# The second copy of each unit's head outputs, moved from ScalarE to a transfer inside SBUF

## The chip, the cores and the metric

The kernel runs on one NeuronCore of a Trainium2 chip. The metric is the device time of one launch in microseconds (us). A core has five instruction streams that run beside each other and meet at semaphores: TensorE (PE in the rows; its weight loads are PEld), VectorE (DVE), ScalarE (ACT), GpSimd (POOL) and SyncE (SP), which here only issues transfers (DMA).

## What is computed

Four sequences of 512 tokens by 256 features pass through four residual layers: latent attention, a feed-forward layer with weights from a 16-entry table, a state-space layer with a scan along the tokens, and the feed-forward layer again. The change is in the attention. Cut to it:

```python
# 16 heads of 128 columns, rank-64 keys and values shared by all heads (absorbed in the kernel)
scores = einsum('bqhd,bkhd->bhqk', q, k) * scale          # causal mask
probs  = softmax(scores)
out    = einsum('bhqk,bkhd->bqhd', probs, v)              # head outputs
x      = x + out.reshape(bs, seq_len, 16 * 128) @ wo.T    # output projection
```

Products run in a reduced fp32 format (fp32r), and each operand that needs more precision is kept as a high part, which is the rounded value, and a low part, which is the rest.

## The kernel before

The attention works in **units**. A unit is one tile of 128 query tokens by one group of G = 4 heads; a sequence has 4 token tiles, so 16 units, and the four sequences have 64. Units 0 to 3 of a sequence belong to token tile 0 and see one block of 128 keys, units 4 to 7 (tile 1) see two blocks, and so on to four in tile 3. Below, "tile 0 of batch 1" means units 0 to 3 of the second sequence.

The order is written out by hand in **slots**. In slot s every engine works on several units at once: `q_up` for unit s, `q_transpose` for s - 2, `scores` and `exp` for s - 3, `p_transpose` for s - 4, `values` for s - 5 and `project` for s - 6 (functions `pe_slot`, `act_slot`, `dve_slot`). The functions wait for each other only by semaphores, and each engine takes its own list strictly in order.

For one unit the steps around the change are these. TensorE transposes the probabilities (`p_transpose`, L1573) once ScalarE has normalised all of them (`normalise`, L866). ScalarE and VectorE split each transposed block into high and low parts (`pt_high` L875, `pt_low` L1205), and `values` (L1587 and L1590) multiplies them by the values into the PSUM bank `bank[6]`: 128 rows by 4 heads by 128 tokens. The matrix `v_hl` holds the high part of the 64 value columns beside the low part, so that rows 0 to 63 of the bank are the product with the high part, rows 64 to 127 that with the low part.

Then the head outputs are split. `out_high` on ScalarE copies the whole bank as `o_a` (L881) and rows 0 to 63 once more as the first half of `o_b` (L883). `out_low` on VectorE puts rows 0 to 63 of the bank less `o_a`, the low part, in the second half of `o_b` (L1211). `project` on TensorE (L1600, L1602) multiplies `o_a` by the weights `wo_a` and `o_b` by `wo_b`. `o_a` and `o_b` have two buffers each, used in turn (`n % 2`). The next unit's first `values` waits for `out_low`, since it overwrites the bank.

`out_high` stands in the middle of `act_slot`: behind it come the squares for the next batch's norm (in tile 0 of the first three batches; L825), the third and fourth `exp` of a later unit (L846), `q_copy` (L853) and the `normalise` calls for which the next `p_transpose` waits. `project` stands near the end of the slot after the one in which `out_high` ran. GpSimd is expanding the table weights all through the attention (L782, L788). SyncE has loaded the inputs by then; its only work during the attention is four loads of state-space weights (`ssm_nat`, L734 to L738), which wait for the last batch's token steps.

Of the kernel before, what the change touches and what calls it, by code (L numbers as in the profile page):

```python
# [4 lines left out]
F32 = mybir.dt.float32  # L5
# [6 lines left out]
P = 128  # L12
BATCH, SEQ, DIM = 4, 512, 256
TB = SEQ // P
CK = DIM // P
HEADS, NOPE, ROPE, DV = 16, 128, 64, 128
QR, KR = 192, 64
# [3 lines left out]
UNITS = TB * (HEADS // G)  # L21
# [59 lines left out]
def token_count(b, k):  # L81

    return 1 + 14 * b + k - 4 * (b - (k == 0)) if b else 1 + k
# [24 lines left out]
def build(nc, x_in, wq_down, wq_up, wq_rope, q_norm_w, wkv_down, kv_norm_w, wkv_up, wk_rope, wo,  # L108
# [3 lines left out]
    with ctx:  # L112
# [89 lines left out]
        o_a = r2("o_a", [P, 2, G, P], F32R)  # L202
        o_b = r2("o_b", [P, 2, G, P], F32R)
# [13 lines left out]
        ssm_nat = nc.alloc_sbuf_tensor_at("ssm_nat", [P, 3, CK, DIM], F32, offset=r2_at)  # L217
# [13 lines left out]
        bank = [nc.alloc_psum_tensor(f"bank{i}", [P, 512], F32) for i in range(8)]  # L231

        def sem(name):
            return ctx.enter_context(nc.semaphore(name))
# [4 lines left out]
        dnat_in, ssm_in, wkn_in, wv_in, wqr_in, wo_in = (  # L239
            sem(n) for n in ("dnat_in", "ssm_in", "wkn_in", "wv_in", "wqr_in", "wo_in"))  # L240
# [17 lines left out]
        at_mm, at_hi, at_lo = sem("at_mm"), sem("at_hi"), sem("at_lo")  # L258
# [3 lines left out]
        recip_s, norm_a, norm_d = sem("recip_s"), sem("norm_a"), sem("norm_d")  # L262
        pt_mm, pt_hi_s, pt_lo_s, pv_mm = sem("pt_mm"), sem("pt_hi_s"), sem("pt_lo_s"), sem("pv_mm")
        o_hi_s, o_lo_s, y_mm = sem("o_hi_s"), sem("o_lo_s"), sem("y_mm")
        x_add, f_add, s_add = sem("x_add"), sem("f_add"), sem("s_add")

        gu_mm, silu_s, hf_s, hhi_s, hlo_s, dn_mm = (
# [432 lines left out]
        @block.sync  # L700
        def _(sp_):
            xr = x_in.rearrange("b (t p) d -> b p t d", p=P)
            outr = out.rearrange("b (t p) d -> b p t d", p=P)
            sp_.dma_start(ident[:, :], c_ident).then_inc(ident_in, 16)
            sp_.dma_start(x[:, 0:TB, :], xr[0]).then_inc(x_in_s[0], 16)
            sp_.dma_start(dn_nat[:, 0, :], wq_down[0:P, :]).then_inc(dnat_in, 16)
            sp_.dma_start(dn_nat[0:QB, 1, :], wq_down[P:QR, :]).then_inc(dnat_in, 16)
            sp_.dma_start(dn_nat[QB:QB + KR, 1, :], wkv_down[:, :]).then_inc(dnat_in, 16)
            wkr = wk_rope.rearrange("(r two) d -> two r d", two=2)
            for two in range(2):  # L710
                sp_.dma_start(dn_nat[32 * two:32 * two + 32, 2, :], wkr[two]).then_inc(dnat_in, 16)
            kvu = wkv_up.rearrange("(h two d) r -> two d h r", h=HEADS, two=2)
            sp_.dma_start(wkn[:, :, :], kvu[0]).then_inc(wkn_in, 16)
            qu = wq_up.rearrange("(h d) q -> d h q", h=HEADS)
            sp_.dma_start(wqu[:, 0:8, 0:QR], qu[:, 0:8, :]).then_inc(wqu_in[0], 16)
            sp_.dma_start(x[:, TB:2 * TB, :], xr[1]).then_inc(x_in_s[1], 16)
            qrr = wq_rope.rearrange("(g hh r two) q -> hh two r g q", hh=2, two=2, r=ROPE // 2)
            for hh in range(2):
                for two in range(2):
                    rows = slice(64 * hh + 32 * two, 64 * hh + 32 * two + 32)  # L720
                    sp_.dma_start(wqr[rows, :, 0:QR], qrr[hh, two]).then_inc(wqr_in, 16)
            for b in range(2, BATCH):
                sp_.dma_start(x[:, b * TB:(b + 1) * TB, :], xr[b]).then_inc(x_in_s[b], 16)
            sp_.dma_start(cos2[:, :, :], c_cos).then_inc(tables_in, 16)
            sp_.dma_start(sin2[:, :, :], c_sin).then_inc(tables_in, 16)
            sp_.dma_start(mask[:, :], c_mask).then_inc(tables_in, 16)
            sp_.dma_start(wqu[:, 8:16, 0:QR], qu[:, 8:16, :]).then_inc(wqu_in[1], 16)
            sp_.dma_start(wo_nat[:, :, :], wo.rearrange("(c p) d -> p c d", p=P)).then_inc(wo_in, 16)
            sp_.dma_start(wv2[:, :, 0, :], kvu[1]).then_inc(wv_in, 16)


            sp_.wait_ge(tok, token_count(BATCH, 0))
            sp_.wait_ge(at_mm, 1 + 3 * BATCH)
            sp_.dma_start(ssm_nat[:, 0, :, :], w_in.rearrange("(c p) d -> p c d", p=P)).then_inc(ssm_in, 16)  # L734
            sp_.dma_start(ssm_nat[:, 2, :, :], w_out.rearrange("(c p) d -> p c d", p=P)).then_inc(ssm_in, 16)
            hpc = P // (DIM // 32)
            for c in range(CK):
                sp_.dma_start(ssm_nat[:, 1, c, :],  # L738
                              w_dt[c * hpc:(c + 1) * hpc, :].unsqueeze(1).to_broadcast([hpc, DIM // 32, DIM]))\
                    .then_inc(ssm_in, 16)  # L740
            for b in range(BATCH):
                for t in range(TB):
                    sp_.wait_ge(f_add, BATCH * TB + b * TB + t + 1)
                    sp_.dma_start(outr[b, :, t, :], x[:, b * TB + t, :]).then_inc(stored, 16)
            sp_.wait_ge(stored, 16 * BATCH * TB)
# [47 lines left out]
        def _(act):  # L793
# [84 lines left out]
            def out_high(b, n):  # L878
                act.wait_ge(pv_mm, b * BLOCKS + blocks_before(n + 1))
                free_after(act, y_mm, b * UNITS + n - 1)  # L880
                nc.scalar.copy(o_a[:, n % 2, :, :].rearrange("p h d -> p (h d)"), bank[6][:, :])\  # L881
                    .then_inc(o_hi_s, 1)
                nc.scalar.copy(o_b[0:KR, n % 2, :, :].rearrange("p h d -> p (h d)"), bank[6][0:KR, :])\  # L883
                    .then_inc(o_hi_s, 1)


# [202 lines left out]
        def _(dve):  # L1089
# [117 lines left out]
                    .then_inc(pt_lo_s, 1)  # L1207

            def out_low(b, n):
                dve.wait_ge(o_hi_s, 2 * (b * UNITS + n) + 2)  # L1210
                nc.vector.tensor_tensor(o_b[KR:P, n % 2, :, :].rearrange("p h d -> p (h d)"), bank[6][0:KR, :],  # L1211
                                        o_a[0:KR, n % 2, :, :].rearrange("p h d -> p (h d)"), ALU.subtract)\
                    .then_inc(o_lo_s, 1)
# [289 lines left out]
        def _(pe):  # L1503
# [88 lines left out]

            def project(b, n):
                g = n % (HEADS // G)
                pe.wait_ge(o_hi_s, 2 * (b * UNITS + n) + 2)
                pe.wait_ge(o_lo_s, 1 + b * UNITS + n + 1)
                if g == 0:
                    pe.wait_ge(x_add, 1 + b * TB + tile_of(n))
                for h in range(G):
                    nc.tensor.matmul(bank[7][:, 0:DIM], o_a[:, n % 2, h, :], wo_a[:, g * G + h, :],  # L1600
                                     start=g == 0 and h == 0, stop=False)
                    last = nc.tensor.matmul(bank[7][:, 0:DIM], o_b[:, n % 2, h, :], wo_b[:, g * G + h, :],  # L1602
                                            start=False, stop=g == HEADS // G - 1 and h == G - 1)
                last.then_inc(y_mm, 1)
# [252 lines left out]
```

## Time and profile before

| | |
|---|---|
| median of 3 runs | 822.56 us (821.38 to 823.37) |
| the profiled execution | 816.43 us, of which the span of its instructions is 814.6 us |
| attention with its units' outputs (first L881 to last) | 78.3 to 558.8 us |
| PE busy over the span | 752.5 us (92%) |
| DVE busy | 675.2 us (83%) |
| ACT busy | 607.2 us (75%) |
| POOL busy | 462.1 us (57%) |
| mean granted TensorE clock | 0.99 of full speed |

All times in the rows count from the start of the span. A line number (L883) is a line of the kernel before. A busy share over the whole span is an average over stages: the feed-forward and state-space stages behind 562 us use ScalarE far less than the attention does, so the rows of single stretches matter here.

### The profile page before, as it was taken

To read this page: it belongs to the slowest core of one execution; us is meant where nothing else is said; L and a number is where in the kernel's file an instruction comes from. 1 tells how busy PE (TensorE), PEld (TensorE's weight loads), DVE (VectorE), ACT (ScalarE), POOL (GpSimd) and SP (SyncE) were. 2 spreads that over 40 slices of the span, in tenths; PEclk is the share of its full clock that TensorE was granted. 3 is DMA by queue.
4 is the path that set the end of the run, shared out by engine and by line. 5 is a ranking of instruction groups with operands and counts; after the bars stand their busy time and mean duration, and the time that the engine had idled before them with its cause. 6 is when DMAs were issued, how large, how long until landed. Compare 5 with 4: busy or idle time off the path is not lost.

```text
span 814.6 us, 15156 instructions
## 1 busy us (share of the span) xinstructions
PE 752.5 (92%) x4556; PEld 648.2 (80%) x4556; DVE 675.2 (83%) x2208; ACT 607.2 (75%) x1508; POOL 462.1 (57%) x388
## 2 busy tenths in 40 slices
PE   4788999999999999999998999999998999999998
PEld 4667888888878788888887888777887788897887
DVE  4986899998899998899998899997775878777643
ACT  2457999987999887999987899895436566674222
POOL 0379999999999999999999999910000000000000
PEclk9988999999999999999999999999999999999999
DMA  9710000000000000000000100000000000000000
GB/s 233 241 53 1 2 1 2 1 1 1 1 2 1 1 2 2 1 2 1 2 1 1 40 2 1 1 1 1 1 1 0 1 1 1 1 1 27 27 27 27
DMA packets 15377, 14.54 MB, mean 18 GB/s; under 512 B 5792, under 2 KB 14432, under 8 KB 15040
## 3 DMA queue, kind: packets, MB, share of 16 engines
q1 hardware_dynamic: 13792, 11.41, 4.8%
q0 software_dynamic: 624, 2.12, 0.8%
q8 instruction: 38, 0.62, 0.3%
q14 instruction: 43, 0.35, 0.1%
q10 hardware_dynamic: 880, 0.04, 0.1%
HBM read 11.46 MB, written 2.10 MB: 17 GB/s over the span
## 4 chain that ended last, share of the span: by engine, by line
PE 57%; DVE 16%; ACT 15%; issue 11%; DMA 1%; DVEq 0%; ACTq 0%; SPq 0%
PE bank L649 11%; PE bank L651 11%; PE bank L650 11%; PE bank L1573 6%; ACT prob L866 5%; ACT prob L846 3%; PE bank L1587 2%; PE bank L1590 2%; DVE pt_lo L1205 2%; ACT pt_hi L875 2%; PE bank L1600 2%; PE bank L1602 2%; PE bank L614 1%; DVE o_b L1211 1%; DVE bias_m L1153 1%
## 5 line engine op out<-in xcount | busy, mean ns | idle before, releaser
L782 POOL TENSOR_SCALAR hot<-raw_gu,lut 128x352 f32<-128x352 int32 x120 | 178.1, 1484 | 12.2
L788 POOL TENSOR_TENSOR total<-total,hot 128x352 f32<-128x352 f32 (+1 forms) x168 | 159.4, 949 | 14.0
L846 ACT ACTIVATE prob<-bank,bias_m 128x128 f32<-128x128 f32 (+3 forms) x256 | 136.2, 532 | 19.4 <-DVE bias_m L1153 19.0
L1153 DVE CUSTOM_DVE_ANT_0 bank<-bank,mask 128x128 f32<-128x128 f32 (+3 forms) x256 | 125.8, 495 | 23.5 <-issue 21.9
L866 ACT ACTIVATE prob<-prob,rden 128x128 f32<-128x128 f32 (+3 forms) x224 | 110.6, 545 | 8.2 <-DVE rden L1188 7.3
L1205 DVE TENSOR_TENSOR pt_lo<-bank,pt_hi 128x512 fp32r<-128x512 f32 x160 | 109.1, 682 | 8.7 <-ACT pt_hi L875 8.3
L1573 PE MATMUL bank<-ident,prob 128*128 128x128 f32 x640 | 99.8, 279 | 15.0 <-ACT prob L866 9.1
L875 ACT CAST pt_hi<-bank 128x512 fp32r<-128x512 f32 x160 | 94.1, 589 | 13.0 <-PE bank L1590 7.2
L1573 PEld LDWEIGHTS bank<-ident,prob 128*128 128x128 f32 x640 | 73.3, 141 | 33.4 <-ACT prob L866 18.6
L649 PE MATMUL bank<-kt_hi,qt_hi 128*128 128x128 f32 (+3 forms) x256 | 87.6, 342 | 3.2 <-ACT prob L846 2.5
L782 POOL TENSOR_SCALAR hot<-raw_dn,lut 128x352 f32<-128x352 int32 (+1 forms) x60 | 87.0, 1451 | 6.1
L651 PE MATMUL bank<-kt_hi,qt_lo 128*128 128x128 f32 (+3 forms) x256 | 83.2, 325 | 0.0
L650 PE MATMUL bank<-kt_lo,qt_hi 128*128 128x128 f32 (+3 forms) x256 | 83.2, 325 | 0.0
L1587 PE MATMUL bank<-pt_hi,v_hl 128*128 128x512 f32 x160 | 68.5, 428 | 3.7 <-issue 3.5
L649 PE MATMUL bank<-xt_hi,gu_hi 128*128 128x512 f32 (+1 forms) x176 | 70.2, 399 | 1.7 <-DVE h_f L1345 1.6
L651 PE MATMUL bank<-xt_hi,gu_lo 128*128 128x512 f32 (+1 forms) x176 | 69.5, 395 | 0.0
L650 PE MATMUL bank<-xt_lo,gu_hi 128*128 128x512 f32 (+1 forms) x176 | 69.4, 394 | 0.0
L1600 PE MATMUL bank<-wo_a,o_a 128*128 128x256 f32 x256 | 67.9, 298 | 0.1
L957 ACT ACTIVATE silu<-bank 128x512 f32<-128x512 f32 x40 | 24.0, 600 | 57.5 <-PE bank L651 57.5
L1590 PE MATMUL bank<-pt_lo,v_hl 128*128 128x512 f32 x160 | 63.6, 398 | 0.3 <-DVE pt_lo L1205 0.2
L1602 PE MATMUL bank<-wo_b,o_b 128*128 128x256 f32 x256 | 63.7, 282 | 0.0
L649 PEld LDWEIGHTS bank<-kt_hi,qt_hi 128*128 128x128 f32 x256 | 49.2, 192 | 13.1 <-ACT prob L846 3.6
(215 smaller groups left out, 2092.7 us busy)
## 6 DMA issues: line engine op xcount, KB each, us to landing
x<-in_L_attn_a_x_dram SPq DMA_DIRECT2D x4, 512.0 KB, 8.1
wo_nat<-in_L_attn_a_wo_dram SPq DMA_DIRECT2D x1, 2048.0 KB, 15.5
out_dram<-x SPq DMA_DIRECT2D x16, 128.0 KB, 1.8
wqu<-in_L_attn_a_wq_up_dram SPq DMA_DIRECT2D x2, 768.0 KB, 8.3
wqr<-in_L_attn_a_wq_rope_dram SPq DMA_DIRECT2D x4, 192.0 KB, 7.0
raw_dn<-in_L_ffn_down_idx_dram POOLq DMA_DIRECT2D x1, 688.0 KB, 6.7
raw_gu<-in_L_ffn_gate_idx_dram POOLq DMA_DIRECT2D x1, 640.0 KB, 5.2
raw_gu<-in_L_ffn_up_idx_dram POOLq DMA_DIRECT2D x1, 640.0 KB, 5.7
```

The costliest lines, as they stand in the source:

```text
L649: nc.tensor.matmul(o, l_hi, r_hi, start=start and k == 0, stop=False)
L650: nc.tensor.matmul(o, l_hi, r_lo, start=False, stop=False)
L651: last = nc.tensor.matmul(o, l_lo, r_hi, start=False, stop=stop and k == n - 1)
L782: nc.gpsimd.tensor_scalar((hot if v else total)[:, 0:n], raw[:, c:c + n], float(v), lut[:, v:v + 1], ALU.is_equal, ALU.mult).then_inc(lut_ ...
L788: nc.gpsimd.tensor_tensor(dst, total[:, 0:n], hot[:, 0:n], ALU.add).then_inc(lut_sum, 1)
L846: nc.scalar.activation(prob[:, n % 2, h, 0:w], bank[2 + h % 2][:, 0:w], ACT.Exp, bias=bias_m[:, n % 2, h:h + 1], scale=-1.0, accum_out=den ...
L866: nc.scalar.activation(prob[:, n % 2, h, 0:w], prob[:, n % 2, h, 0:w], ACT.Copy, scale=rden[:, n % 2, h:h + 1]).then_inc(norm_a, 1)
L875: nc.scalar.copy(pt_hi[:, c % 2, :, :].rearrange("p h d -> p (h d)"), bank[4 + c % 2][:, :])\
L1153: nc.vector.tensor_tensor_reduce(out=bank[2 + h % 2][:, 0:w], in0=bank[2 + h % 2][:, 0:w], in1=mask[:, TB * P - w:TB * P], scale=1.0, scal ...
L1205: nc.vector.tensor_tensor(pt_lo[:, c % 2, :, :].rearrange("p h d -> p (h d)"), bank[4 + c % 2][:, :], pt_hi[:, c % 2, :, :].rearrange("p h ...
L1573: last = nc.tensor.transpose(bank[4 + c % 2][:, h * P:(h + 1) * P], prob[:, n % 2, h, j * P:(j + 1) * P], ident[:, :])
L1587: nc.tensor.matmul(bank[6][:, :], v, pt_hi[:, c % 2, :, :].rearrange("p h d -> p (h d)"), start=j == 0, stop=False)
```

## The change

`out_high` makes only the first copy, `o_a`. The first half of `o_b` is filled by a DMA that SyncE issues, from rows 0 to 63 of `o_a` to rows 0 to 63 of `o_b`, 64 partitions of 2 KB, 128 KB in all, once per unit. It carries a semaphore per buffer, `o_dup[0]` and `o_dup[1]`, and `project` waits for it besides the two waits that it had. `out_low` waits for `o_a` alone. The counts of `o_hi_s` are halved accordingly. SyncE takes its list in order too, so the four loads of `ssm_nat` are now put behind the transfer of the last batch's first unit.

```diff
+            def load_ssm():
+                sp_.wait_ge(tok, token_count(BATCH, 0))
+                sp_.wait_ge(at_mm, 1 + 3 * BATCH)
...
+            def duplicate(b, n):
+
+                sp_.wait_ge(o_hi_s, b * UNITS + n + 1)
+                sp_.dma_start(o_b[0:KR, n % 2, :, :].bitcast(F32), o_a[0:KR, n % 2, :, :].bitcast(F32)).then_inc(o_dup[n % 2], 16)
+
+            for b in range(BATCH):
+                for n in range(UNITS):
+                    duplicate(b, n)
+                    if b == BATCH - 1 and n == 0:
+                        load_ssm()
...
                 nc.scalar.copy(o_a[:, n % 2, :, :].rearrange("p h d -> p (h d)"), bank[6][:, :])\
                     .then_inc(o_hi_s, 1)
-                nc.scalar.copy(o_b[0:KR, n % 2, :, :].rearrange("p h d -> p (h d)"), bank[6][0:KR, :])\
-                    .then_inc(o_hi_s, 1)
...
             def out_low(b, n):
-                dve.wait_ge(o_hi_s, 2 * (b * UNITS + n) + 2)
+                dve.wait_ge(o_hi_s, b * UNITS + n + 1)
...
             def project(b, n):
                 g = n % (HEADS // G)
-                pe.wait_ge(o_hi_s, 2 * (b * UNITS + n) + 2)
+                pe.wait_ge(o_hi_s, b * UNITS + n + 1)
+                pe.wait_ge(o_dup[n % 2], 16 * ((b * UNITS + n) // 2 + 1))
                 pe.wait_ge(o_lo_s, 1 + b * UNITS + n + 1)
```

On ScalarE one row of each slot goes. The place shown is in batch 2, where tile 0 ends, first before the change:

```order
L846 ACTIVATE prob,den<-bank,bias_m 128x256
L875 CAST pt_hi<-bank 128x512
L881 CAST o_a<-bank 128x512
L883 CAST o_b<-bank 64x512
L825 ACTIVATE squares,ms<-cd 128x192
L825 ACTIVATE squares,ms<-cd 128x64
L846 ACTIVATE prob,den<-bank,bias_m 128x256
L875 CAST pt_hi<-bank 128x512
L846 ACTIVATE prob,den<-bank,bias_m 128x256
L853 COPY q_tok<-bank 128x4x64
L866 ACTIVATE prob<-prob,rden 128x256 x4
```

and the same place with the change, where the line numbers are those of the changed kernel (L894 is the copy `o_a`, L879 the normalising):

```order
L859 ACTIVATE prob,den<-bank,bias_m 128x256
L888 CAST pt_hi<-bank 128x512
L894 CAST o_a<-bank 128x512
L838 ACTIVATE squares,ms<-cd 128x192
L838 ACTIVATE squares,ms<-cd 128x64
L859 ACTIVATE prob,den<-bank,bias_m 128x256
L888 CAST pt_hi<-bank 128x512
L859 ACTIVATE prob,den<-bank,bias_m 128x256
L866 COPY q_tok<-bank 128x4x64
L879 ACTIVATE prob<-prob,rden 128x256 x4
```

Nothing else is reordered there; seven rows stand between the copy and the normalising, and each may start one copy earlier. On SyncE the list behind the first loads was, before the change:

```order
L729 DMA wv_139<-in_L_attn_a_wkv_up_dram 128x16x64
L734 DMA ssm_nat<-in_L_attn_b_W_in_dram 128x2x256
L735 DMA ssm_nat<-in_L_attn_b_W_out_dram 128x2x256
L738 DMA ssm_nat<-in_L_attn_b_W_dt_dram 128x1x256 x2
L744 DMA out_dram<-x 128x256 x16
```

and is now this (L730 is the last load of the start, L757 the stores of the output):

```order
L730 DMA wv_139<-in_L_attn_a_wkv_up_dram 128x16x64
L747 DMA o_b<-o_a 64x512 x49
L736 DMA ssm_nat<-in_L_attn_b_W_in_dram 128x2x256
L737 DMA ssm_nat<-in_L_attn_b_W_out_dram 128x2x256
L740 DMA ssm_nat<-in_L_attn_b_W_dt_dram 128x1x256 x2
L747 DMA o_b<-o_a 64x512 x15
L757 DMA out_dram<-x 128x256 x16
```

Forty-nine transfers now stand ahead of the state-space weights and fifteen behind them. TensorE's and VectorE's lists have the same rows as before; only what the first L1600 of each unit waits for has grown.

## Rows read from the trace of the kernel before

**Rows 1.** The page: busy time of each engine, and the chain's shares
```profile
PE 752.5 (92%) x4556; PEld 648.2 (80%) x4556; DVE 675.2 (83%) x2208; ACT 607.2 (75%) x1508; POOL 462.1 (57%) x388
...
PE 57%; DVE 16%; ACT 15%; issue 11%; DMA 1%; DVEq 0%; ACTq 0%; SPq 0%
```

**Rows 2.** Stretches: length, busy of PE, PEld, DVE, ACT, POOL, clock, DMA
```profile
78.20:103.60 25.40, 23.90 (x158) 20.87 (x157) 22.96 (x94) 25.19 (x89) 23.64 (x20) 1.00 0.01 2
103.60:134.80 31.20, 28.58 (x182) 24.74 (x181) 30.03 (x109) 30.20 (x81) 29.06 (x24) 1.00 0.01 2
...
202.40:228.00 25.60, 24.38 (x166) 21.77 (x165) 22.73 (x97) 25.35 (x89) 23.75 (x21) 1.00 0.01 2
228.00:259.30 31.30, 29.00 (x182) 24.63 (x182) 30.53 (x109) 30.23 (x81) 29.07 (x25) 1.00 0.00 1
...
294.30:327.60 33.30, 31.48 (x204) 27.27 (x204) 30.21 (x102) 27.34 (x74) 30.99 (x25) 1.00 0.01 2
327.60:352.80 25.20, 24.38 (x166) 21.68 (x165) 21.41 (x92) 25.07 (x89) 23.46 (x19) 1.00 0.00 1
352.80:382.40 29.60, 27.76 (x175) 24.20 (x174) 28.39 (x107) 29.27 (x79) 27.46 (x24) 1.00 0.01 2
...
451.10:474.50 23.40, 22.75 (x149) 19.61 (x148) 22.23 (x100) 22.19 (x70) 21.72 (x19) 1.00 0.03 8
474.50:502.10 27.60, 26.70 (x168) 23.35 (x166) 26.70 (x98) 27.39 (x74) 25.65 (x22) 1.00 0.01 1
```

**Rows 3.** Groups of ACT instructions: the two copies
```profile
L881 ACT CAST o_a<-bank 128x512 fp32r<-128x512 f32 x64 | 38.9, 608 | 4.8 <-PE bank L1590 4.5
L883 ACT CAST o_b<-bank 64x512 fp32r<-64x512 f32 x64 | 37.9, 592 | 0.0
```

**Rows 4.** Waits from 100 to 560 us: us in total, times, longest
```profile
PEld bank L1573 <- ACT prob L866: 16.7, 34, 1.1
```

**Rows 5.** Timeline of a slot in batch 2, tile 0: start, us, engine
```profile
346.56 0.61 ACT L883 CAST o_b<-bank 64x512 fp32r<-64x512 f32 x1
...
347.04 0.40 ACT L825 ACTIVATE squares<-cd 128x192 f32<-128x192 f32 x1
...
349.45 1.72 ACT L866 ACTIVATE prob<-prob,rden 128x256 f32<-128x256 f32 x4
...
351.22 0.42 PEld L1573 LDWEIGHTS bank<-ident,prob 128*128 128x128 f32 x4 [0.56 <-ACT prob L866]
```

**Rows 6.** Timeline of ACT behind L883 in batch 2, tile 3
```profile
427.77 0.69 ACT L846 ACTIVATE prob<-bank,bias_m 128x512 f32<-128x512 f32 x1 [0.22 <-DVE bias_m L1153]
...
428.73 0.59 ACT L875 CAST pt_hi<-bank 128x512 fp32r<-128x512 f32 x1 [0.19 <-PE bank L1573]
```

**Rows 7.** Timelines: copy and project of the first unit of batch 3, and of the second-last
```profile
451.21 0.59 ACT L881 CAST o_a<-bank 128x512 fp32r<-128x512 f32 x1
...
457.74 0.33 PE L1600 MATMUL bank<-wo_a,o_a 128*128 128x256 f32 x1
...
552.57 0.60 ACT L881 CAST o_a<-bank 128x512 fp32r<-128x512 f32 x1
...
558.05 0.28 PE L1600 MATMUL bank<-wo_a,o_a 128*128 128x256 f32 x1
```

**Rows 8.** The same for the last unit of the attention
```profile
558.25 0.58 ACT L881 CAST o_a<-bank 128x512 fp32r<-128x512 f32 x1 [1.32 <-PE bank L1590]
...
560.14 0.19 PEld L1600 LDWEIGHTS bank<-wo_a,o_a 128*128 128x128 f32 x1 [0.34 <-issue]
```

**Rows 9.** Line L744, the output's stores of 128 KB each, SBUF to HBM
```profile
DMA to landing us min/median/max: 1.7/1.8/3.9
```

**Rows 10.** DMA issues: engine, count, KB, us to landing
```profile
cos<-in_cos_dram SPq DMA_DIRECT2D x1, 128.0 KB, 8.1
```

**Rows 11.** Where batch 3 begins: PE's wait, and the stretch behind it
```profile
447.24 0.77 PE L1587 MATMUL bank<-pt_hi,v_hl 128*128 128x512 f32 x1 [1.76 <-issue]
...
447.00:450.00 3.00, 2.76 (x11) 2.60 (x12) 1.87 (x13) 1.75 (x7) 2.82 (x3) 0.54 0.59 165
```

More of the change, by code:

```diff
@@ L264, in build @@
         o_hi_s, o_lo_s, y_mm = sem("o_hi_s"), sem("o_lo_s"), sem("y_mm")
+        o_dup = [sem(f"o_dup{k}") for k in range(2)]
         x_add, f_add, s_add = sem("x_add"), sem("f_add"), sem("s_add")
@@ L729, in _ @@
             sp_.dma_start(wv2[:, :, 0, :], kvu[1]).then_inc(wv_in, 16)
[L732 to L740, printed above, removed]
+            def load_ssm():
+                sp_.wait_ge(tok, token_count(BATCH, 0))
+                sp_.wait_ge(at_mm, 1 + 3 * BATCH)
+                sp_.dma_start(ssm_nat[:, 0, :, :], w_in.rearrange("(c p) d -> p c d", p=P)).then_inc(ssm_in, 16)
+                sp_.dma_start(ssm_nat[:, 2, :, :], w_out.rearrange("(c p) d -> p c d", p=P)).then_inc(ssm_in, 16)
+                hpc = P // (DIM // 32)
+                for c in range(CK):
+                    sp_.dma_start(ssm_nat[:, 1, c, :],
+                                  w_dt[c * hpc:(c + 1) * hpc, :].unsqueeze(1).to_broadcast([hpc, DIM // 32, DIM]))\
+                        .then_inc(ssm_in, 16)
+            def duplicate(b, n):
[6 more added lines that the diff above has]
+                        load_ssm()
             for b in range(BATCH):
```

## The prediction

> **What bounds the kernel now.** I read the page first. TensorE is busy 92% of the span and has 57% of the chain that ended last; ScalarE is busy 75% and has 15% of the chain [rows 1]. By that alone, relieving ScalarE looks idle. But the share is an average, so I next read the stretches of the attention, cut by token tile [rows 2]. There the picture changes. In tile 0 of the first three batches ScalarE is busy 25.19 of 25.40 us, 25.35 of 25.60 and 25.07 of 25.20: it has no gap left, while TensorE idles 1.50, 1.22 and 0.82 us. In tile 1 ScalarE is busy 30.20 of 31.20, 30.23 of 31.30 and 29.27 of 29.60, TensorE idles 2.62, 2.30 and 1.84 us, and VectorE, the third busy engine, idles 1.17, 0.77 and 1.21 us. In tile 3 ScalarE has room: 27.34 of 33.30 us. So ScalarE sets or shares the pace in tiles 0 and 1, and TensorE in tiles 2 and 3, where it is busy throughout but for short waits.
>
> The waits say through which door this comes: from 100 to 560 us TensorE's loads for `p_transpose` (L1573) waited 16.7 us for ScalarE's normalising (L866), in 34 waits of at most 1.1 us [rows 4]. That is the sum on which a faster ScalarE can work, and it is the largest of TensorE's waits.
>
> **The change part by part.** *The copy that goes.* L883 takes 592 ns on average and there are 64, 37.9 us busy [rows 3]. Instructions of ScalarE overlap, though: in the slot shown L883 starts at 346.56 and the next instruction at 347.04, so what leaves the engine's line is 0.47 us a unit, about 30 us over the attention. Per tile of four units that is 4 x 0.47 = 1.88 us.
>
> *How much of it TensorE gets back.* One slot of tile 0 shows the best case. From L883 at 346.56 ScalarE runs without a gap up to the last of four L866, which start at 349.45 and end at 351.17, and TensorE's load for L1573 at 351.22 had waited 0.56 us for it [rows 5]. Everything from L883 on can move forward by 0.47 us, so nearly all of that wait goes. In tile 3 it is different: behind L883 ScalarE stands still 0.22 us for VectorE's row maximum and then 0.19 us for TensorE, 0.41 us together [rows 6]; a copy less makes these two waits longer and moves nothing. I price tiles 2 and 3 at nothing. What hides the gain there is that ScalarE's own waits follow directly, and its idle of 5.96 us in the tile 3 stretch [rows 2] says that this cover is thick.
>
> For tiles 0 and 1 I work out a ceiling for each stretch: the stretch can't shrink by more than ScalarE frees (1.88 us), nor by more than the idle time of whichever other engine is busier [rows 2]. In tile 0 that engine is TensorE: 1.50, 1.22 and 0.82 us in batches 0 to 2, and 0.65 us in batch 3 (22.75 busy of 23.40). In tile 1 it is VectorE: 1.17, 0.77 and 1.21 us, and 0.90 us in batch 3 (26.70 of 27.60, the same for TensorE). The sum is 8.24 us. The floor is nothing: the other engines' small waits could just be moved about. The best case of the slot is not the rule (in batch 3 ScalarE is busy only 22.19 of 23.40 us in tile 0, so it has gaps of its own), but the first three batches are near it. I take two thirds of the ceiling, **5.5 us**.
>
> *The low part.* `out_low` now waits for one copy instead of two. It stands last in VectorE's slot, and VectorE is at it later than the copy in nearly every slot, so I count nothing; the half microsecond on the last two units is in the next term.
>
> *The transfer.* The trace has no transfer inside SBUF. The nearest rows are the output's stores: the same 128 KB from SBUF on the same queue, 1.7 us at least and 1.8 us at the median from issue to landing, 3.9 at most [rows 9]. The slowest of this size is the load of a table among many others at the start, 8.1 us [rows 10]. I take 1.8 us, since the queues are empty in the attention, and allow 0.15 us for SyncE to wake and for TensorE to see the semaphore: 1.95 us.
>
> The Trainium skill speaks against small transfers here: "DMA: Bandwidth & Descriptors", section "Anatomy of one DMA — SWDGE (gpsimd) path", gives a fixed cost of about 2.0 us per transfer, measured on GpSimd's path, and its fit would make 2.3 us of 128 KB. The store's row is on SyncE's path and somewhat below that. By the page's figure each transfer costs four times the copy that it replaces, and the last unit would pay 0.5 us more than in my sum.
>
> The cover is the distance from `o_a`'s end to the unit's first L1600. For the first unit of batch 3 it is 451.80 to 457.74, 5.9 us; for the second-last unit of all 552.57 + 0.60 to 558.05, 4.9 us [rows 7]. Slots are shortest in batch 3's tile 0 and at the end, so these are about the least that there are. A transfer of 1.95 us is hidden with 3 us to spare 63 times. Not so at the last unit: `o_a` ends at 558.83, and TensorE's load started at 560.14 [rows 8]. With the transfer it starts at 558.83 + 1.95 = 560.78, **0.6 us later**, and behind it stand the last weight transposes and the feed-forward layer's first products, for which everybody waits. Between 0 (a transfer as short as the copy path) and 1.5 us more are possible, and 6.9 us at the 8.1 us of the slow row.
>
> *What is queued behind the new waits.* On TensorE the first L1600 waits for one semaphore more; these are taken while earlier products run, so nothing. On SyncE only the state-space loads and the output's stores stand behind the transfers. The loads now start after the first unit's `o_a` of batch 3, at 451.80, later than before; they are wanted only in the feed-forward stage, behind 562 us. The next transfer behind them has 5.9 us of cover: nothing. GpSimd and its tables are not touched.
>
> *Sum.* -5.5 + 0.6 = **-4.9 us**. Against the profiled execution (816.43 us) that is 811.5 us. The median of the runs shown is 822.56 us, 6.1 us above the profiled one; I take the difference off that: **817.7 us**, 0.6% less. What a measurement can tell from no change is about 0.2%, 1.6 us.
>
> **The rivals.** *Nothing comes of it* (25%). TensorE and VectorE take up the slack: TensorE idles only 3 to 6% in tile 0, VectorE 2 to 4% in tile 1 [rows 2], and the waits for L866 turn into waits for VectorE's row maximum or `pt_low`. For it: wherever ScalarE has a gap, the other end of it is VectorE. Against it: three stretches in which ScalarE has none. The time is then 822.56 + 0.6 = 823.2 us, and with a little gain 821 to 824.
>
> *More than the ceiling* (8%). My stretches' idle times are after TensorE's modelled ends; if all the 16.7 us of waits for L866 [rows 4] shortened by 0.3 us each, 34 x 0.3 = 10 us, it would be 813 us.
>
> *The transfer is late in every unit, slower* (17%). The place is L1600 of the tile 0 units. The point from which it decides is a landing 5.9 us behind `o_a` [rows 7]; the page has such a row, 8.1 us [rows 10]. Then the 16 units of tile 0 lack up to 8.1 + 0.15 - 5.9 = 2.3 us each. Since a late product also delays the next unit and gives it cover, I count between once per batch (9 us) and every unit (37 us), 15 us: 822.56 - 4.9 + 15 = 833 us. A mean of some 4 us would cost only the last unit (2.8 us) and leave the gain at 2. Against it: the queues are all but empty in the attention, a DMA share of 0.01 or less in six of the eight stretches of tiles 0 and 1 [rows 2], and the 8.1 us row stood among the loads of the start.
>
> *TensorE's clock.* At the start of batch 3 TensorE waited 1.76 us, and the granted clock of the stretch from 447 to 450 us was 0.54, that is mostly 1.2 GHz instead of 2.4 [rows 11]. Products there take twice as long. That wait is for VectorE's split of the values, not for ScalarE, so I expect both to stay. If the dip goes or one more of 3 us comes, it is worth some 1.5 us either way; the range holds it.
>
> **How the numbers follow.** The forecast, a gain of 2 to 8 us, has 50%: 814.5 to 820.5 us. With the others the range that holds 8 in 10 is 812.5 to 824.0 us; what is left out is the slow rival's bulk and the top of the gain. Faster by over 0.2% is the forecast and the larger gain, 58%; within 0.2% most of the first rival, 26%; slower 16%.
>
> **What the changed profile would show.** ScalarE's busy time falls by some 37 us, and in tile 0 stretches it is no longer full. The waits of L1573 for L866 fall from 16.7 to about 8 to 11 us. The tile 0 and 1 stretches of batches 0 to 2 shrink by about 0.7 us each, those of tiles 2 and 3 by nothing. The transfers land 1.7 to 2.3 us from issue, and no L1600 but the last unit's waits for one. If L1600 shows waits in tile 0, the transfer is what I sized wrongly; if L1573 now waits for VectorE instead, the ceiling was.

## The result, and the profile of the changed kernel

| | before | changed |
|---|---|---|
| median | 822.33 us (816.0 to 824.47, 20 executions) | 816.27 us (20 executions; 19 of them from 813.8 to 818.62) |
| ratio | | 0.9941 (0.9921 to 0.9961) |
| profiled execution | 816.43 us, span 814.6 us | 816.2 us, span 814.4 us |
| ScalarE busy | 607.2 us | 583.2 us |

The changed kernel is 0.6% faster, 6.1 us by the medians, where 4.9 us were forecast. (A twentieth execution of it took 2534 us; such lone ones came with the kernel before too and are left out of ranges and groups; without it the median is 816.20 us.) The two profiled executions, however, are equal to 0.2 us. So the time was read rightly in total, and the two traces side by side show almost none of the gain. That contradiction is what the experiments are about.

The page of the changed kernel, to be held against [rows 1] and, for the transfer, [rows 9]. The last row's end is KB each and the median us from issue to landing:

```profile
PE 752.6 (92%) x4556; PEld 650.8 (80%) x4556; DVE 674.3 (83%) x2208; ACT 583.2 (72%) x1444; POOL 462.5 (57%) x388
...
PE 60%; DVE 17%; issue 13%; ACT 9%; DMA 1%; DVEq 0%; ACTq 0%; SPq 0%
...
o_b<-o_a SPq DMA_DIRECT2D x64, 128.0 KB, 2.2
```

ScalarE's share of the chain fell from 15% to 9%, and TensorE, issue and VectorE took it over: most of what ScalarE no longer does on that chain has been replaced by something else that took as long. ScalarE is busy 24.0 us less over the run. The transfer lands after 2.2 us; over all 64 it is 2.2 at least and 2.8 us at most.

The stretches of tile 0 and tile 1 of batches 0 to 2, in that order, against [rows 2]:

```profile
80.20:104.70 24.50, 23.42 (x159) 20.76 (x158) 21.99 (x94) 23.76 (x85) 22.74 (x20) 1.00 0.11 23
203.60:228.70 25.10, 24.01 (x165) 21.80 (x165) 22.15 (x95) 24.04 (x85) 23.28 (x20) 1.00 0.10 22
326.70:351.20 24.50, 24.01 (x166) 21.74 (x165) 20.74 (x92) 23.93 (x85) 22.73 (x20) 1.00 0.11 23
104.70:136.10 31.40, 28.60 (x182) 24.76 (x181) 29.96 (x109) 28.77 (x77) 29.27 (x24) 1.00 0.08 18
228.70:259.00 30.30, 28.46 (x183) 24.80 (x182) 29.11 (x109) 28.62 (x77) 28.25 (x23) 1.00 0.09 19
351.20:381.70 30.50, 27.96 (x174) 24.06 (x173) 29.42 (x107) 27.91 (x75) 28.37 (x24) 1.00 0.09 19
```

Tile 0 shrank from 25.40, 25.60 and 25.20 us to 24.50, 25.10 and 24.50. Tile 1 went from 31.20, 31.30 and 29.60 us to 31.40, 30.30 and 30.50: one shorter by 1.0 us, two longer by 0.2 and 0.9. ScalarE is busy 28.77 of 31.40 us there, no longer full, and the time is not less. From the first `o_a` to the last the attention takes 476.8 us instead of 480.0. Of these 3.2 us the changed execution lost 2.0 before the attention began, in which the change has no part, and 1.0 at the last unit (below). That makes the two spans equal. A single pair can't carry more than that: from the last `o_a` to the end of the span it is 256.2 to 257.7 us in the profiles of kernels whose last unit has no transfer, 1.5 us apart by themselves.

The waits in the changed kernel from 100 to 560 us (total us, times, longest), against [rows 4]:

```profile
ACT prob L859 <- DVE bias_m L1164: 25.8, 45, 1.6
...
PEld bank L1584 <- ACT prob L879: 16.6, 32, 1.1
```

TensorE still waits 16.6 us for the normalising (L1584 and L879 are the former L1573 and L866). The forecast 8 to 11 us is plainly missed. What grew is ScalarE's own wait for VectorE's row maximum; in the kernel before it was 12.3 us in the same stretch.

The last unit in the changed kernel, against [rows 8]:

```profile
557.04 0.58 ACT L894 CAST o_a<-bank 128x512 fp32r<-128x512 f32 x1 [1.32 <-PE bank L1601]
...
559.94 0.19 PEld L1612 LDWEIGHTS bank<-wo_a,o_a 128*128 128x128 f32 x1 [1.35 <-issue]
```

From `o_a`'s end at 557.62 to TensorE's load it is 2.32 us; 1.95 were forecast. From `o_a`'s start it is 2.90 us, and before it was 560.14 - 558.25 = 1.89. The last unit pays 1.0 us.

### The profile page after: what moved, and what is told of

Its sections match the earlier page's. It is cut to its first block, busy times and chain, and to the rows that moved or that the text cites. A ratio compares the mean times of both kernels' runs of the same rounds, so it can differ in the third digit from the quotient of the medians.

```text
span 814.4 us, 15172 instructions
## 1 busy us (share of the span) xinstructions
PE 752.6 (92%) x4556; PEld 650.8 (80%) x4556; DVE 674.3 (83%) x2208; ACT 583.2 (72%) x1444; POOL 462.5 (57%) x388
## 4 chain that ended last, share of the span: by engine, by line
PE 60%; DVE 17%; issue 13%; ACT 9%; DMA 1%; DVEq 0%; ACTq 0%; SPq 0%
PE bank L650 11%; PE bank L652 11%; PE bank L651 11%; PE bank L1584 6%; ACT prob L879 4%; DVE pt_lo L1216 3%; PE bank L1598 2%; PE bank L1601 2%; PE bank L1612 2%; PE bank L1614 2%; DVE o_b L1222 2%; PE bank L615 2%; DVE bias_m L1164 2%; PE bank L1547 1%; ACT prob L859 1%
## 5 line engine op out<-in xcount | busy, mean ns | idle before, releaser
L879 ACT ACTIVATE prob<-prob,rden 128x128 f32<-128x128 f32 (+3 forms) x224 | 110.3, 541 | 9.5 <-DVE rden L1199 8.0
L1584 PE MATMUL bank<-ident,prob 128*128 128x128 f32 x640 | 99.6, 278 | 14.3 <-ACT prob L879 9.1
L1584 PEld LDWEIGHTS bank<-ident,prob 128*128 128x128 f32 x640 | 73.5, 141 | 31.9 <-ACT prob L879 18.4
```

The source lines that it names most:

```text
L879: nc.scalar.activation(prob[:, n % 2, h, 0:w], prob[:, n % 2, h, 0:w], ACT.Copy, scale=rden[:, n % 2, h:h + 1]).then_inc(norm_a, 1)
L1584: last = nc.tensor.transpose(bank[4 + c % 2][:, h * P:(h + 1) * P], prob[:, n % 2, h, j * P:(j + 1) * P], ident[:, :])
```

## The experiments

Kernels that mix copies and transfers all have the same frame, a function `how(n)` of the unit's number in the whole run; only its line differs:

```diff
+def how(n):
+    return "act" if n == BATCH * UNITS - 1 else "dma"
...
             def duplicate(b, n):
+                if how(b * UNITS + n) != "dma":
+                    return
...
+                if how(b * UNITS + n) == "act":
+                    nc.scalar.copy(o_b[0:KR, ...], bank[6][0:KR, :]).then_inc(o_cp, 1)
```

Each unit's waits follow its kind. Their line numbers differ from those above, by up to 30 lines. The experiments were measured in three series, each with the kernel before beside it: its medians were 822.40, 821.63 and 822.39 us. Where medians of different series are compared, the text says so.

### Is the gain there at all, and is it ScalarE's?

**The kernel before once more**, no edit.

> The kernel before, unchanged, run once more for the clock and span of each of its executions. Two theories of the 6 us between the medians. 'ScalarE': the freed ScalarE time shortens tiles 0 and 1 of the first three batches (the two profiles show 3.2 us less from the first to the last copy of o_a), and the transfer costs 1 us at the last unit; then executions of equal clock differ by 2 to 3 us between the kernels and the rest of the 6 us is the clock. 'All in the clock': at equal granted clock before and after are the same within 1 us, and the kernel before has a lower mean clock by some 0.007. If instead its clocks are like the changed kernel's (0.981 to 0.994) and its times still fall in two groups near 817.5 and 823.5 us, the groups are two ways in which the slots lock to each other.

Measured: 822.62 us (816.08 to 824.73, 12 executions), ratio 0.9998 (0.9966 to 1.003). The times are not spread evenly. Of the kernel before there are 107 executions in all, with those beside the other experiments but without two odd ones (847 and 2534 us). 39 lie from 814.3 to 819.9 us with median 817.1, 68 from 821.2 to 825.1, and none in between. The TensorE clock does not divide them: at a granted clock of 0.990 there are 816.0 and 817.6 us and several from 821.2 to 822.9. (Over the 87 executions that have it on record its mean is 0.989 in the low group and 0.986 in the high one, with most values common to both; whether the rest is cause or effect is not shown.) The kernel before was profiled first in the low group (816.43 us), this time in the high one (824.12 us), and the changed kernel, but for the lone one, has no execution above 818.62 us. So two profiles of one group could not show the gain, and the step of my sum that added 6.1 us to go from the profiled execution to the median took a group for an offset.

**No second copy at all** after the first two units:

```diff
+    return "act" if n < 2 else "none"
```

> The second copy is made for the first two units alone and never again, by nobody: o_b's first half keeps old values, there is no transfer and no wait for one. 'ScalarE' expects the change's gain and the 1 us that the transfer costs at the last unit on top: ratio to before 0.992, some 815 us. A theory by which transfers themselves matter in the attention (SBUF traffic, SyncE) expects a larger step from the changed kernel than 1 us.

Measured: 815.35 us (812.68 to 818.01), ratio 0.9928 (0.9901 to 0.9955). With neither copy nor transfer it is 0.9 us less than the changed kernel. That equals the last unit's price in the rows (next but one), though two medians of different series could not show it by themselves. Inside the attention the 64 transfers cost nothing that shows: 476.3 us from the first `o_a` to the last, against 476.8, one profile each.

**Copy and transfer both**, the transfer behind the copy, writing the same bytes. Here `duplicate` has no early return, so all 64 transfers run, and `project` waits for both:

```diff
+    return "act"
...
-                sp_.wait_ge(o_hi_s, b * UNITS + n + 1)
+                sp_.wait_ge(o_cp, b * UNITS + n + 1)
```

> ScalarE makes both copies as before the change and a transfer writes the same bytes over the second one; TensorE waits for it. This is the price of the transfers alone. 'ScalarE': ratio 1.001 to 1.002, from the last unit's wait, which is now behind two copies, 1.5 us; the other 63 transfers cost nothing. If transfers inside SBUF slow the engines, the stretches of the attention get longer and the ratio is above 1.003.

Measured: 824.03 us (818.47 to 826.52, 11 executions), ratio 1.0043 (1.0009 to 1.0077). So it is not the transfer, nor the changed list of SyncE, that brings the gain: with them and with the copy the time is the old one plus 2.4 us (0.7 to 6.3 by the interval). The last unit, whose transfer now starts behind two copies, explains 1.5 of it: from `o_a`'s start to TensorE's load it is 3.37 us instead of 1.89. `project` shows a wait at one unit alone, 1.6 us. Without the copy the gain is there, transfer or not; with the copy it is not. So it comes from relieving ScalarE.

**The last unit's copy back on ScalarE**, the frame as shown above.

> The changed kernel, but the last unit's second copy is made by ScalarE again. The wait of TensorE for the last transfer (1.35 us in the profile, 0.34 before the change) goes: 1.0 us less than the changed kernel, ratio to before 0.993. If the feed-forward stage hides that wait, it equals the changed kernel.

Measured: 814.61 us (812.22 to 817.79), ratio 0.9932 (0.9904 to 0.9959). The last unit in its trace:

```profile
557.57 0.59 ACT L906 CAST o_a<-bank 128x512 fp32r<-128x512 f32 x1 [1.32 <-PE bank L1618]
...
558.05 0.58 ACT L909 CAST o_b<-bank 64x512 fp32r<-64x512 f32 x1
...
559.53 0.19 PEld L1632 LDWEIGHTS bank<-wo_a,o_a 128*128 128x128 f32 x1 [0.41 <-issue]
```

From `o_a`'s start to the load it is 1.96 us, against 1.89 before the change. The price of the last unit is thus 2.90 - 1.96 = 0.9 us, and this is the best complete version; its ratio's interval overlaps with that of the changed kernel, but the rows show what it saves.

### Which tiles

**Transfers in tiles 0 and 1 only**, and **in tiles 2 and 3 only**:

```diff
+    return "dma" if tile_of(n % UNITS) < 2 else "act"
```

> Transfers only for units of token tiles 0 and 1, ScalarE's copy for those of tiles 2 and 3 (also the last unit). 'ScalarE in tiles 0 and 1' expects the whole gain and no loss at the end: ratio to before 0.992 to 0.994. If the gain comes from tiles 2 and 3 or from the end, it is half or less: 0.997 or more.

```diff
+    return "dma" if tile_of(n % UNITS) >= 2 else "act"
```

> Transfers only for units of token tiles 2 and 3, ScalarE's copy in tiles 0 and 1. 'ScalarE' (its time counts in tiles 0 and 1 alone) expects no gain and the last unit's loss: ratio 1.001. 'Collisions' expects something between, since moving ScalarE anywhere shifts the pattern: up to half of the gain, 0.997 to 1.001, possibly in two groups as before.

Measured: tiles 0 and 1 817.05 us (813.35 to 824.91), ratio 0.9955 (0.9921 to 0.9988), 11 of 12 executions in the low range; tiles 2 and 3 823.12 us (814.26 to 827.38), ratio 1.0035 (1.0 to 1.0071), 10 of 12 in the high one. The gain comes with tiles 0 and 1, as forecast, and tiles 2 and 3 alone, which also pay for the last unit, give none.

### What the two groups are

The two costliest groups of VectorE in the attention whose duration varies are the last addition of the rotary step (L1172, both operands in SBUF) and VectorE's share of the normalising (L1196, from SBUF to SBUF). Groups from 80 to 560 us (count, busy us, mean ns), first of the kernel before in its low execution:

```profile
L1172 DVE TENSOR_TENSOR q_tok<-q_tok,q_rot 128x256 f32<-128x256 f32 x59 | 30.8, 521 | 2.0
...
L1196 DVE TENSOR_SCALAR prob<-prob,rden 128x512 f32<-128x512 f32 x32 | 18.1, 608 | 0.0
```

the same kernel in its high execution:

```profile
L1172 DVE TENSOR_TENSOR q_tok<-q_tok,q_rot 128x256 f32<-128x256 f32 x59 | 34.7, 589 | 2.0
...
L1196 DVE TENSOR_SCALAR prob<-prob,rden 128x512 f32<-128x512 f32 x32 | 21.0, 698 | 0.0
```

and the changed kernel:

```profile
L1183 DVE TENSOR_TENSOR q_tok<-q_tok,q_rot 128x256 f32<-128x256 f32 x59 | 29.5, 499 | 2.0
...
L1207 DVE TENSOR_SCALAR prob<-prob,rden 128x512 f32<-128x512 f32 x32 | 17.4, 585 | 0.0
```

The sums are 48.9, 55.7 and 46.9 us. The same sum is 55.1 us in the profile of copy-and-transfer and 58.9 in that of tiles 2 and 3 (both high), and 48.0, 48.4 and 47.2 without the copy, with the last copy back, and with tiles 0 and 1 (all low). All other groups of VectorE above 10 us keep their mean within some ns; a few small ones from SBUF to SBUF vary too (L1121, 426 and 424 ns here, 277 in the next kernel). One L1172 takes 424 ns at least and 1207 at most: something holds it now and then for up to 0.8 us. In the attention GpSimd runs its table expansion almost without a pause. Where the two meet, in the high execution:

```profile
252.08 0.95 POOL L788 TENSOR_TENSOR total<-total,hot 128x352 f32<-128x352 f32 x1
...
252.13 1.19 DVE L1172 TENSOR_TENSOR q_tok<-q_tok,q_rot 128x256 f32<-128x256 f32 x1
```

The held addition ends at 253.32, 0.29 us behind the end of GpSimd's. From 80 to 560 us the low execution has 18 of 59 that take over 0.47 us, the high one 25 and the changed kernel 15, and every one of them started while an instruction of GpSimd was running. Those that started in one of its additions all end 0.27 to 0.30 us behind its end. Those held by one of its scalings of 1.5 us started in its first 0.31 us, and end 0.6 us before its end.

The next pair leaves 14 of the 16 table entries out, in the kernel before and in the changed one:

```diff
...
-                    for v in range(LUT):
+                    for v in range(2):
...
```

> The kernel before, with GpSimd's table expansion cut from 16 entries to 2 (the feed-forward weights are then partial sums, so the output is another one); GpSimd is done early in the attention instead of working through nearly all of it. The two profiles of the kernel before differ by 4.5 us in the attention, and the additions q_tok<-q_tok,q_rot on VectorE (424 ns at best) take 1207 ns at worst. Theory 'collisions': VectorE's operations that read SBUF twice sometimes wait for GpSimd, the kernel before falls in one of two patterns of such collisions, and the change keeps it out of the worse one. It expects here one group of times instead of two, below 814 us, with these additions at 424 to 450 ns behind GpSimd's end. Theory 'ScalarE alone' expects the two groups to stay, since GpSimd is not on the path.

> The changed kernel with the same cut of GpSimd's work, to be set beside the kernel before with that cut. 'Collisions' expects the difference between the two to be far less than 6 us: the freed ScalarE time of tiles 0 and 1 (2 to 3 us) less 1 us for the last unit's transfer, so 1 to 2 us. 'ScalarE alone' expects the 6 us to stay.

Measured: 805.22 us (803.26 to 806.17, 6 executions), ratio 0.9831 (0.9789 to 0.9874), and 803.01 us (801.03 to 804.63, 6), ratio 0.9808 (0.9769 to 0.9847). The same VectorE group of the kernel before with little GpSimd work:

```profile
L1172 DVE TENSOR_TENSOR q_tok<-q_tok,q_rot 128x256 f32<-128x256 f32 x59 | 25.1, 425 | 2.0
...
L1196 DVE TENSOR_SCALAR prob<-prob,rden 128x512 f32<-128x512 f32 x32 | 14.0, 481 | 0.0
```

Between 80 and 560 us the longest L1172 takes 0.43 us, the six times lie within 3 us, in one group instead of two, and the kernel is 17 us faster (16.4, by the medians of its series). Nearly all of that lies in the attention: from the first `o_a` to the last it takes 466.6 us, against 480.0 in the low execution and 484.5 in the high one. The two groups of VectorE account for most of these 13.4 and 17.9 us: their sum is 39.1 us here, 9.8 less than in the low and 16.6 less than in the high one. So GpSimd's work beside VectorE costs that much, by holding VectorE up, and the groups go with it. The Trainium skill gives a mechanism, in "SBUF — State Buffer", section "SBUF: two separate sides": VectorE and GpSimd share a pair of ports, and an instruction of VectorE with two SBUF inputs (against a GpSimd one that reads SBUF), or in a two-port mode, has to wait until GpSimd's whole instruction is through, or the reverse. The trace agrees in the instructions that it hits, and in the size for GpSimd's additions of 0.95 us. It does not agree for the scalings of 1.5 us: an L1172 held by one is through 0.6 us before it ends, so the hold is far shorter than the whole instruction. That it also decides between the two groups is tested by moving GpSimd's work as a whole by one more instruction of 1.5 us at its start:

```diff
-            n_hot = n_sum = 0
+            flat = raw_gu[:, :, :].rearrange("p t d -> p (t d)")
+            nc.gpsimd.tensor_scalar(total[:, 0:GC], flat[:, 0:GC], 0.0, lut[:, 0:1], ALU.is_equal, ALU.mult).then_inc(lut_hot, 1)
+            pool.wait_ge(lut_hot, 1)
+            n_hot, n_sum = 1, 0
```

> The kernel before, with one more GpSimd instruction (1.5 us) ahead of the table expansion, so that everything GpSimd does in the attention comes 1.5 us later against the other engines; its cycle of two instructions is 2.4 us. If the two groups of times (near 817 and 823 us) are set by where GpSimd's cycle stands when VectorE's operations come, the mix changes, to mostly the low group or to still higher times. If the engines always slide into the same patterns on their own, the mix stays: about three in four executions near 823 us, ratio 1.000.

> The changed kernel with the same shift. If its lack of a high group is luck of the phase, the group near 823 us appears here. If less ScalarE work keeps the slots out of the worse pattern whatever the phase, it stays at 814 to 818 us, ratio 0.993 to 0.995.

Measured: the kernel before becomes faster by doing more, 818.2 us (813.43 to 828.11, 12 executions), ratio 0.9954 (0.9923 to 0.9986); 9 executions lie below 819 us and 3 at 822.8 or above. The changed kernel takes 817.53 us (815.58 to 819.98, 9), ratio 0.9951 (0.9928 to 0.9974), all below 820 us. So where GpSimd stands relative to VectorE can weigh nearly as much as the change under study: 4.2 us by the medians, 1.1 to 6.3 by the interval. Where the high executions lose is known, too: of the 4.5 us by which the profiled one is longer from the first `o_a` to the last, 3.6 lie in tiles 2 and 3 of batches 1 and 2 and in tile 0 of batch 3, and only 0.4 in the tile 0 stretches that the change shortens (below). What makes the changed kernel keep the low group at either position is not shown: that it needs the relief in tiles 0 and 1 is measured, the way from there to fewer collisions is not.

### What ScalarE's relief is worth by itself

The pair with little GpSimd work is free of collisions but for the first 16 us of the attention, so its stretches can be compared to some hundredths of a us. The difference of the medians is 2.2 us, with six executions each that lie 2.9 and 3.6 us apart; the rows are the firmer ground. Measured from `o_a`'s start to `o_a`'s start, tile 0 takes 25.23, 25.22 and 25.21 us before and 24.35, 24.54 and 24.55 changed: 0.88, 0.68 and 0.66 us less, 2.2 us in all. Tile 1 takes 30.02, 30.02 and 28.94 before and 30.26, 29.98 and 28.93 changed: no gain, and 0.24 us more in batch 0. Tiles 2 and 3 and batch 3 are equal within 0.06 us, but for 0.5 us less in the very last stretch. This half microsecond comes at the very end, where the last two distances between `o_a`s shrink from 7.10 and 5.67 us to 6.79 and 5.44. In the first of them ScalarE sets the pace once more: the normalising starts 2.46 instead of 2.77 us behind `o_a`, and the two `pt_high` behind it, for which VectorE stands idle, as much earlier. In the second it is `out_low`, which starts 0.86 instead of 1.10 us behind `o_a`, and with it the next `values`. The rows of batch 1's tile 0 and tile 1, before with little GpSimd work:

```profile
200.10:225.30 25.20, 24.40 (x166) 21.71 (x166) 21.85 (x97) 25.07 (x89) 0.00 (x0) 1.00 0.01 2
225.30:255.40 30.10, 28.36 (x182) 24.87 (x181) 28.43 (x109) 29.98 (x82) 0.00 (x0) 1.00 0.00 1
```

and changed with little GpSimd work:

```profile
198.20:222.70 24.50, 23.95 (x166) 21.71 (x165) 21.39 (x95) 23.91 (x85) 0.00 (x0) 1.00 0.11 23
222.70:252.70 30.00, 28.29 (x182) 24.88 (x181) 28.35 (x109) 28.48 (x77) 0.00 (x0) 1.00 0.09 19
```

The second row of each is the lesson of this case. ScalarE is busy 29.98 of 30.10 us, as full as in tile 0; TensorE and VectorE have 1.7 us to spare; 1.5 us of ScalarE's work go, and the stretch is as long as it was. The rows of one slot tell why. Before, in tile 1 of batch 1:

```profile
232.14 0.61 ACT L881 CAST o_a<-bank 128x512 fp32r<-128x512 f32 x1
...
232.61 0.59 ACT L883 CAST o_b<-bank 64x512 fp32r<-64x512 f32 x1
...
232.87 0.60 PE L1573 MATMUL bank<-ident,prob 128*128 128x128 f32 x4
...
233.09 0.48 ACT L846 ACTIVATE prob<-bank,bias_m 128x256 f32<-128x256 f32 x1
...
233.55 0.58 ACT L875 CAST pt_hi<-bank 128x512 fp32r<-128x512 f32 x1
```

and changed, the same slot:

```profile
229.53 0.61 ACT L894 CAST o_a<-bank 128x512 fp32r<-128x512 f32 x1
...
230.12 0.47 ACT L859 ACTIVATE prob<-bank,bias_m 128x256 f32<-128x256 f32 x1
...
230.28 0.60 PE L1584 MATMUL bank<-ident,prob 128*128 128x128 f32 x4
...
230.91 0.59 ACT L888 CAST pt_hi<-bank 128x512 fp32r<-128x512 f32 x1 [0.23 <-PE bank L1584]
```

The `exp` does move forward, from 0.95 to 0.59 us behind `o_a`. But the `pt_high` behind it needs the next block's `p_transpose`, which TensorE does at its own pace: 0.73 us behind `o_a`'s start in the first, 0.75 in the second. So `pt_high` starts 1.41 us behind `o_a` before and 1.38 changed, now with a wait of 0.23 us in front. With `p_transpose` as its releaser everything after it stands where it stood: the first normalising starts 2.58 us behind `o_a` in both, and TensorE's wait for it is unchanged (three waits, 2.1 us, in this stretch of both). The other slots of the stretch are alike: ScalarE now has four such waits there, 1.4 us in all, which is nearly all of the 1.5 us of work that went. The copy lay in the shadow of `p_transpose`: ScalarE was never idle, yet the copy's half microsecond was on no path. ScalarE's waits from 100 to 545 us say the same, before with little GpSimd work:

```profile
ACT prob L846 <- DVE bias_m L1153: 6.9, 22, 0.8
ACT pt_hi L875 <- PE bank L1573: 5.1, 18, 0.5
```

and changed with little GpSimd work:

```profile
ACT prob L859 <- DVE bias_m L1164: 16.3, 33, 0.9
ACT pt_hi L888 <- PE bank L1584: 13.7, 35, 0.6
```

These two grow by 9.4 and 8.6 us, 18 of the 30 us that ScalarE was given. In tile 0 a unit has one block only, there is no second `pt_high` to hold, and a part comes through: in batch 1 TensorE's waits for the normalising fall from 1.3 to 0.9 us there.

Two last kernels, both with the short expansion:

```diff
+    return "dma" if n < 3 * UNITS and tile_of(n % UNITS) == 0 else "act"
```

> With short GpSimd work: transfers only for the twelve units of token tile 0 of the first three batches, ScalarE's copy for the other 52. The two profiles with short GpSimd work differ by 0.88, 0.69 and 0.66 us in exactly these stretches and by nothing in tiles 1 to 3. If that is all of ScalarE's part, this kernel has it whole and pays nothing at the end: 805.2 - 2.2 = 803.0 us, attention's tile 0 stretches at 24.4 to 24.6 us. If tiles 1 to 3 gave something, it lies above 804.

```diff
+    return "act" if n == BATCH * UNITS - 1 else "dma"
```

> The changed kernel with short GpSimd work and the last unit's copy on ScalarE again. Without GpSimd's collisions the price of the last transfer is seen alone: 1.0 us below the changed kernel with short GpSimd work (803.0), so 802.0 us.

Measured: 802.79 us (801.22 to 804.38, 5 executions), ratio 0.9762 (0.9731 to 0.9794), and 802.2 us (800.96 to 803.07, 4), ratio 0.9755 (0.9725 to 0.9785). In us, twelve transfers give 805.22 - 802.79 = 2.4 us, as much as all 64 do (2.2). The last copy put back gives 0.8 us more, as at the full table. These medians come from another series than the pair's and from five and four executions, so the rows have to bear it out, and they do. From the first `o_a` to the last the kernel before takes 466.6 us, twelve transfers 464.4 and all of them 463.8: tile 0 of the first three batches holds 2.2 us, and the rest is the half microsecond of the last units, which the last unit's price outweighs. The ratios to the kernel before are not used across series here, since that kernel's share of the high group differs from one to the next.

## Why the prediction was right, and where it was not

- **The total was right, its main term was not what filled it.** The term "5.5 us, two thirds of the ceiling" is the step that was mis-sized: ScalarE's relief measures 2.2 us in tile 0 and 0.5 us at the last units (`out_low`'s part included), 2.7 in all. Net of the last unit's 0.9 us that leaves about 2 us, as the pair without collisions shows (2.2). The rest of the measured 6.1 us, some 4, is a thing that the sum did not contain: the changed kernel keeps out of the group of executions at 821 us and above, in which 68 of 107 of the kernel before lie. The two parts do not add up so neatly in the single times: within the low group it is 817.1 against 816.3 us, only 0.8 between the kernels, and the step from the high group to the low one is 5.8 us. That the gain came out within 1.2 us of the forecast is thus luck.
- **Tile 0** was given 1.50, 1.22 and 0.82 us at the ceiling, two thirds of it 2.4 us; measured 2.2. That part of the argument held, with ScalarE as the pace there. In batch 3, where the ceiling gave 0.65 us more, the stretch stayed (23.18 and 23.15 us in the pair).
- **Tile 1** was given 1.17, 0.77 and 1.21 us at the ceiling; measured no gain. The ceiling asked whether ScalarE was full and the others had room. It should have asked, at one slot, what stands behind the copy: a `pt_high` that `p_transpose` releases, so that it can move by 0.03 us and not by 0.47.
- **Tiles 2 and 3 at nothing**: right but for 0.3 us behind the third-last unit. Shown alone they give no gain (1.0035), and the other stretches are equal within 0.06 us.
- **`out_low` at nothing**: wrong by 0.2 us, at the second-last unit. The prediction counts the half microsecond of the last two units "in the next term", and the next term does not hold it.
- **ScalarE's busy time** fell by 24.0 us and not by 37, which is the copies' summed duration. The prediction's own 0.47 us a unit gives 30; the other 6 may be overlap of neighbours that is lost where a wait now stands between them, which was not traced.
- **The waits for L866 as the door of the gain**: wrong in the main. They stayed at 16.6 us, and in the pair without collisions went from 16.9 to 15.7 (100 to 545 us), by as little as tile 0 would have it. They are the end of a loop that runs through both engines, and not a sum on which a faster ScalarE could draw.
- **The transfer** was sized at 1.8 us by the nearest row and landed after 2.2, and the 0.15 us allowed beside it came out at 0.1; the last unit pays 0.9 to 1.0 us instead of 0.6. The estimate of 2.3 us for 128 KB from the fit in the Trainium skill ("DMA: Bandwidth & Descriptors", section "Anatomy of one DMA — SWDGE (gpsimd) path") was the nearer figure, though this transfer is SyncE's. The cover of 63 units held: no `project` but the last waited.
- **The rivals.** "Nothing comes of it" was right about tile 1 in that the freed time turned into waits, though there they are for TensorE's `p_transpose` (1.4 of 1.5 us) and not for the row maximum, as it had them, and wrong about tile 0 of the first three batches. The late transfer did not come. (Had the landing taken 4 us, by the prediction's own terms 2.7 us of gain would have been left, not 2; and the DMA share is 0.01 or less in seven of its eight stretches, not six. Neither changes the forecast.)
- **GpSimd is not touched** was true of its list, and overlooked that VectorE's durations hang on it.

## What to carry to other kernels

An engine that is busy 100% of a stretch is not by that its bound: take one slot, put the instruction behind the edited one beside its releaser on the other engine, and see how far it can move before that releaser holds it. Where a profiled execution lies well off the median, look at the single times before anything is worked out: two groups a few us apart can be worth more than the change, and a profile shows only one of them. A copy moved to a transfer had 2.2 us of latency here for a copy of 0.59 us, so leave the last one, for which everybody waits, on the engine.

## What the runs showed that I had not expected

- GpSimd's elementwise work in SBUF beside the attention costs 17 us of 822, nearly all of it through VectorE: 425 ns becomes 521 to 589 ns in the mean and 1207 ns at most for an addition of two SBUF operands, 481 becomes 608 to 698 ns for a scaling from SBUF to SBUF. Instructions that read PSUM keep their time (L1205 682 and 680 ns with the full expansion, 683 with the short one).
- An addition of VectorE caught by a GpSimd addition ends 0.27 to 0.30 us behind it; caught by a GpSimd scaling of 1.5 us, it is through 0.6 us before the scaling ends.
- A delay of GpSimd by 1.5 us made the kernel before faster, 818.2 instead of 822.39 us.
- A transfer of 128 KB inside SBUF from 64 partitions took 2.2 us, against 1.8 us for a store of as many bytes from 128 partitions. Which of the two differences makes the 0.4 us was not tried.
